# Hybrid block on one core: the router's marks and inversions leave out the step without a whole chunk, and the sum into X moves to the seventh chunk

## The reference

```python
x = x + attention(layernorm(x))        # 16 heads of 8, window of 32
x = x + ffn(layernorm(x))              # the mixture stage
x = x + mixer(layernorm(x)) # two selective scan layers
x = x + ffn(layernorm(x))              # the mixture stage again
```

```python
out = swiglu(x, shared_gate_up, shared_down)          # inner width 938, all tokens
probs = softmax(x @ gate_weight.T)                    # 8 experts
top_p, sel = top_k(probs, 2);  top_p /= top_p.sum(-1) + 1e-8
for e in range(8):
    out += cw[..., e:e+1] * swiglu(x, experts_gate_up[e], experts_down[e])
```

## Time and profile before

| what | before |
|---|---|
| median of 3 runs | 2160.12 us (2157.04 to 2160.7) |
| the profiled execution, its own time | 2158.89 us |
| its span, first to last instruction | 2157.1 us |
| PE busy with matmuls | 2008.0 us (93%) |
| DVE, ACT, POOL busy | 1497.0, 1201.5, 1440.7 us |
| mean granted TensorE clock | 0.977 of full |

### The profile page before, as it was taken

The page is one execution under the profiler, slowest core; times in us unless marked ns, Lnnn a source line. Parts: engine busy times, 40 slices in busy tenths (PEclk is TensorE's granted clock), DMA queues, the critical chain, the costliest instruction groups (busy, mean ns, idle before and its releaser), DMA issues. The chain is left out here.

```text
span 2157.1 us, 42455 instructions
## 1 busy us (share of the span) xinstructions
PE 2008.0 (93%) x14350; PEld 1535.7 (71%) x14351; DVE 1497.0 (69%) x2749; ACT 1201.5 (56%) x2399; POOL 1440.7 (67%) x972
## 2 busy tenths in 40 slices
PE   7998999999999988989988889898789999999998
PEld 5886448999999545656655556565554489999994
DVE  6887684333333579999999999999976833333335
ACT  5775423222222279999989888989844132222222
POOL 6774005777767249999999999989940067777670
PEclk9999999999999989999999999989899999999999
DMA  8000100000001422332322323222233000000014
GB/s 304 0 1 11 30 1 20 26 24 25 24 24 26 111 96 90 101 106 93 100 89 100 99 89 98 100 91 97 83 138 143 1 22 26 24 26 24 24 25 121
DMA packets 72198, 141.91 MB, mean 66 GB/s; under 512 B 9835, under 2 KB 43629, under 8 KB 69910
## 3 DMA queue, kind: packets, MB, share of 16 engines
q1 hardware_dynamic: 62998, 121.86, 16.9%
q0 software_dynamic: 9088, 18.63, 3.0%
HBM read 123.81 MB, written 16.65 MB: 65 GB/s over the span
## 5 line engine op out<-in xcount | busy, mean ns | idle before, releaser
L2269 POOL TENSOR_TENSOR m_seen<-m_state,experts 128x1024 f32<-128x1024 f32 x256 | 600.7, 2369 | 59.8 <-DVE m_state L2323 54.2
L2323 DVE TENSOR_TENSOR_SCAN m_state<-experts,ps 128x512 f32<-128x512 f32 x448 | 540.1, 1235 | 0.5 <-PE ps L1860 0.5
L1877 PE MATMUL ps<-ident,m_seen 128*128 128x128 f32 x2048 | 278.8, 281 | 36.9 <-POOL m_seen L2269 36.9
L1877 PEld LDWEIGHTS ps<-ident,m_seen 128*128 128x128 f32 x2048 | 243.2, 145 | 75.8 <-POOL m_seen L2269 54.9
L2082 ACT ACTIVATE experts<-delta,experts 128x512 f32<-128x512 f32 x448 | 291.3, 713 | 1.0 <-DVE delta L2349 0.5
L1591 POOL COPY f_weights<-experts 128x1898 f32 x142 | 252.3, 1777 | 23.8 <-issue 23.5
L1414 PE MATMUL first_up_ps<-f_xT,f_weights 128*128 128x128 f32 x1988 | 241.4, 275 | 1.7 <-issue 1.7
L1414 PE MATMUL ps<-zu,f_weights 128*128 128x128 f32 x1988 | 241.4, 275 | 1.7 <-issue 1.7
L1414 PEld LDWEIGHTS first_up_ps<-f_xT,f_weights 128*128 128x128 f32 x1988 | 233.2, 192 | 2.5 <-issue 2.5
L1414 PEld LDWEIGHTS ps<-zu,f_weights 128*128 128x128 f32 x1988 | 233.2, 192 | 2.5 <-issue 2.5
L2303 DVE TENSOR_TENSOR ps<-m_delta_u,ps 128x512 f32<-128x512 f32 x286 | 193.4, 676 | 15.4 <-PE ps L1835 15.1
(11 more groups left out here) (451 smaller groups left out, 3904.2 us busy)
## 6 DMA issues: line engine op xcount, KB each, us to landing
experts<-m_rows SPq DMA_DIRECT2D x144, 512.0 KB, 3.6
experts<-in_experts SPq DMA_DIRECT2D x17, 1461.0 KB, 18.6
tokens<-f_rows SPq DMA_DIRECT2D x8, 512.0 KB, 5.3
f_rows<-expert_out SPq DMA_DIRECT2D x8, 512.0 KB, 7.0
f_cols<-expert_out SPq DMA_DIRECT2D x8, 512.0 KB, 7.0
out<-X SPq DMA_DIRECT2D x4, 512.0 KB, 3.2
X<-in_x SPq DMA_DIRECT2D x4, 448.0 KB, 5.9
f_xin<-tokens,f_take POOLq DMA_INDIRECT x71
```

The costliest lines, as they stand in the source:

```text
L1877: mm = pe.matmul(Y[:, i // 2, at:at + P], seen[:, n % SEEN, h, i * P:(i + 1) * P], ident[:], is_transpose=True, start=(n == 0 and at == 0) ...
L2269: pool.tensor_tensor(seen[:, n % SEEN], state[:, n % RING], c_rep[:, Q % C_RING, n % C_GROUP, :].unsqueeze(1).to_broadcast([P, HALF, SEG]) ...
L2323: dve.tensor_tensor_scan(state[:, n % RING, h, :], decay_, drive_, before_, ALU.mult, ALU.add).then_inc(s_state, 1)
```

## The change

It does three things, in both mixture stages.

- The marks begin one step earlier (k = 13, step 24), and steps with c = 7 are left out, on DVE for marks and on PE for inversions. Marks stand in steps 24 to 30, 32 to 38, 40 and 41; inversions, each one such step after its mark, in 25 to 30, 32 to 38, 40, 41 and 42; `find_holders` in step 42 instead of 41.
- `place_weights` leaves the list of the router and is run in step 31 (c = 7 of group 3) instead of 24.
- The sum of group g - 1 into X moves in the early groups from step c = 2 to c = 6, ahead of that step's mark. The late groups keep c = 2.

```diff
-                    COUNT_AFTER, MARK_AFTER = 6, 6
+                    COUNT_AFTER, MARK_AFTER = 6, 5
...
+                    HOLD = WHOLE - AHEAD
+                    MARKED_AT = [k for k in range(NC + MARK_AFTER, GROUPS * NC) if k % NC != HOLD][:BATCHES + 1]
+                    PLACED_AT = NC + NC + HOLD
...
-                                      count_tiles, find_bases, find_places, pick_places, split_places, find_experts, place_weights]
+                                      count_tiles, find_bases, find_places, pick_places, split_places, find_experts]
...
-                                if follows and c == 2:
+                                if follows and c == (2 if g in LATE_GROUPS else WHOLE - 1):
                                     end(g - 1)
...
                                     k = (g - 1) * NC + c
-                                    b = k - len(router)
-                                    if b < 0:
+                                    if k < len(router):
                                         router[k]()
-                                    elif b < BATCHES:
-                                        mark(b)
-                                    elif b == BATCHES:
+                                    elif k in MARKED_AT[:BATCHES]:
+                                        mark(MARKED_AT.index(k))
+                                    elif k == MARKED_AT[BATCHES]:
                                         find_holders()
+                                    elif k == PLACED_AT:
+                                        place_weights()
...
-                                    b = (g - 2) * NC + c - 1 - MARK_AFTER
-                                    if 0 <= b < BATCHES:
-                                        invert(b)
+                                    k = (g - 1) * NC + c
+                                    if k in MARKED_AT[1:]:
+                                        invert(MARKED_AT.index(k) - 1)
```

## The result

| what | before | after |
|---|---|---|
| median, 6 runs each on one chip | 2160.66 us (2157.04 to 2163.14) | 2149.69 us (2144.95 to 2155.13) |
| ratio | | 0.995, 95% interval 0.9938 to 0.9961 |
| span of the profiled execution | 2157.1 us | 2153.4 us |
| its own time | 2158.89 us | 2155.13 us |

The change makes the kernel 11.0 us faster by the medians, and by 8.4 to 13.4 us by the interval (0.0039 and 0.0062 of 2160.66). On another chip the changed kernel's median was 2150.01 us against 2160.5, a ratio of 0.9953 (0.9937 to 0.9969). The profiled execution of the changed kernel is its slowest of six, so its span must not be set against that of before. What the change does is read from single stretches.

A forecast was written before the change was run, and what follows sets the result against it. PE was taken to set the pace, losing time in waits for marks. Per stage -2.27 - 1.13 - 0.52 + 0.25 = -3.67 us, twice -7.34, with the clock's -1.71 in all -9.05: 2150.5 us, range 2146.5 to about 2154.8.

The forecast's parts named there:

- Step 31: In each mixture stage, without an inversion in this step PE's wait for the mark goes: -2.27 us a stage.
- step 39: In each mixture stage, without an inversion here PE's wait behind the tail's four matmuls goes: -1.13 us a stage.
- The sum: Sum into X, moved from steps 26 and 34: gives back 0.52 us a stage, costs 0.25 in step 32.
- place_weights: Run in step 31, it delays step 32's mark behind the group's transposes: cost taken as 0, bound 0.35 us.
- The slack of steps 14 to 24: DVE's idle time in steps 17 and 24 covers the moved sum: cost nothing, else up to 0.6 us once.
- find_holders: One step later by number, ends about 0.8 us earlier; slack before the first gathered tile stays 2.3 us or more.
- The clock: Second mixture stage, behind step 31: with PE's idle time gone the clock stays at its upper level, -1.71 us.
- the clock might give less: Rival: the second stage's fall is the run's or comes back elsewhere; only -7.34 us, about 2152.2 us; chance 0.16.
- DVE becomes the bound: Rival: at the group's end sum, place_weights and mark collide, each stage keeps 0.35 + 0.6 us; 2152.4 us; chance 0.06.
- the waits only move: Rival: PE waits for marks around steps 31 and 39 as long as before; 2158 to 2161 us; chance 0.09.
- the mixer stage gives it all back: Rival: with the earlier start more of the mixer stage falls to half clock; 2164.5 us, slower; chance 0.05.
- the prediction's own signs of being wrong: In the trace: waits for L1103 elsewhere, PE waiting at the first tile, or mixer stage off 840 us by over 2.

The follow-up runs named there:

- its own experiment: The changed kernel with place_weights in step 39 instead of step 31; measured stages of 56.57 and 56.56 us.
- The slow mark: The changed kernel with the first comparison in the mark of step 30 run four more times; measured stages of 60.79 and 61.15 us.

## Why the prediction was right

**The bound.** PE set the pace, and its waits for marks were the loss. All the changes of a stage's length in the experiments follow PE's waits, and the falls of the clock behind them, to about a tenth of a microsecond. What was gained before the expert part reached the end: the two stretches from the first gathered tile on (to the mixer stage, and to the end) took 425.8 and 422.3 us before and 425.9 and 422.3 after.

**Step 31, -2.27 us, and step 39, -1.13 us.** Both waits are gone, and no other has come. They were measured together: 60.11 - 56.84 = 3.27 us with the sum left at c = 2, against 3.40. For step 39 alone the experiment has 1.64 with the sum ahead of its mark, where 1.13 + 0.60 = 1.73 was expected. The missing 0.1 us is partly seen: behind the tail the gate and up matmuls hold PE for 318.06 - 316.24 = 1.82 us instead of the 1.76 with an inversion between (291.36 to 293.98 is 2.62, less 0.86 of the down matmuls).

**The sum.** It gives back 0.52 us and costs 0.25. Measured is 0.28 net, and the one cost, PE's late inversion in step 32, is there with 0.25. The version with the sum at c = 7 saves just this.

**place_weights.** Taken as 0, with a bound of 0.35: 0, by its own experiment. The reason given was right too: the mark of step 32 ends at 299.29 + 0.82 = 300.11, while PE is still at the transposes that begin at 300.00, and the inversion starts at 300.44. It was cheaper on DVE than its four instructions' 0.73 us suggest, since the product behind it started 0.63 us after it (297.61 - 296.98).

**The slack of steps 14 to 24.** It held: the product of step 24 began at once behind its gate, and the stages show no wait of PE there. In step 17 DVE was idle for 0.23 us instead of the 0.58 of the earlier trace rows.

**find_holders.** I had it ending 0.8 us earlier. It ended at 328.17 against 328.18, but this execution was 0.85 us late already at step 25 (279.15 against 278.30), so this is as worked out. The slack of at least 2.3 us was conservative: by the experiment with find_holders three steps later it is 7.54 - 3.74 = 3.8 us. One step more was hidden, three were not.

**The clock, -1.71 us.** The mechanism was right and its size a matter of chance, as the Trainium skill's page "TensorE: Matmul & The Clock Gate", Part 1, would have it with a phase that runs free of the kernel; the traces agree, by the two outcomes of one wait of 2.12 us. But the rival that I drew from this, that the clock might give less, put it wrongly: the fall is neither the run's own nor always there. With four falls in six waits it cost the kernel before an estimated 2 x 0.67 x 1.7 = 2.3 us on average, 0.6 more than my one trace showed.

**The sum in all.** -7.34 - 1.71 = -9.05 us was forecast, -8.8 us stand in the stage lengths of the two first traces, and with 2.3 us for the clock the traces give 2 x 3.55 + 2.3 = -9.4. The medians say -11.0 and -10.5; both intervals hold 9.4. The forecast of 2150.5 us lies 0.8 us above the median of 2149.69, and that it is so near is in part luck: the terms of the sum account for about 9 of the 11.0 us, and no trace shows where the rest would come from, since outside the two stages the traces of the changed kernel are not shorter than those of before. Single executions of the changed kernel spread over 10.2 us, and those of before over 6.1. The prediction put the 3.66 us between its three runs down to the mixer stage alone, and that was wrong. Over the thirteen traces the mixer stage varies by 7.7 us, but all that stands ahead of step 25 in the first stage varies too, from 278.3 to 283.3 us. To the 3.66 us of three runs I had given too much weight.

**The rivals.** That DVE becomes the bound, that the waits only move, and that the mixer stage gives it all back are out. The slow mark shows what the first of them would look like: 2.9 us more of DVE in one place and the stage is about as long as before. One of the prediction's own signs of being wrong did come up in the first trace: the mixer stage, measured alike, took 4.0 us more than before, where 2 was the bound. The second trace of the changed kernel, with 833.7 us, takes it back. The sign was badly chosen: the kernel before alone varies by 3.6 us there, and the 840 us of the earlier trace rows were a round stretch around a stage of 837.3.

## What to carry to other kernels

When side work is dealt out over the steps of a main loop, an irregular step is not a free slot for a consumer: what it waits for is made behind the main work of the step before, and there is no main work in it to hide the wait. Let the producer use such a step (the sum, the small bookkeeping) and let the consumer pass over it. Where TensorE waits as long as the waits here that were followed by a fall of the clock (2.12 us and more), price the wait at its length plus a share of what the fall cost, and compare stretches of the trace, not the spans of two executions, when the effect is smaller than their spread.

## What the runs showed of the hardware that I had not expected

An equal wait of 2.12 us was followed by 1.2 instead of 2.4 GHz in four of six cases, one of 2.17 us at another place in ten of thirteen, and those of 2.72 to 4.05 us in six of six. Behind waits of 1.06, 1.40 and 1.66 us it never happened, in ten cases and 26 of the 1.40 us. A fall behind a wait of 2.12 or 2.72 us cost about 1.7 us, one that began within the wait 1.3, and those at the first gathered tile 0.6 and 0.9; why these two cost less was not tested. And the length of the mixer stage varied from 833.7 to 841.4 us over thirteen traces of kernels that don't differ there, with the time at half clock as at most a part of the cause.
